# A macaron block on one Trainium2 core: the first feed-forward starts with a slot of 256 rows chosen from 512 tokens, the activation is rewritten, and the software DMA queue is drained inside the kernel

## What is computed

```python
x = x + 0.5 * ffn(layernorm(x))
x = x + attention(layernorm(x))          # 16 heads, recurrent "ABC" attention over chunks
x = x + 0.5 * ffn(layernorm(x))          # the same weights as the first

def ffn(x):                              # 2 experts, hidden size 2048
    probs = softmax(x @ w_router.T)
    e = argmax(probs); w = probs[e]
    h = x @ w_fc[e].T
    a = square(where(h >= 0, h, 0.5 * h))
    return w * (a @ w_proj[e].T)
```

## Time and profile before

| | |
|---|---|
| median of 3 runs | 2006.97 us (2006.1 to 2009.6) |
| the profiled execution's own time | 2002.07 us |
| its span, first to last instruction | 2000.3 us |
| mean granted TensorE clock | 0.992 of full speed |
| PE / weight loads / DVE / ACT / POOL busy | 95% / 80% / 70% / 33% / 14% |
| DMA over the span | 181.32 MB, 91 GB/s |

### The profile page before, as it was taken

The page is one execution under the profiler, slowest core; times in us unless marked ns, Lnnn a source line. Parts: engine busy times, 40 slices in busy tenths (PEclk is TensorE's granted clock), DMA queues, the critical chain, the costliest instruction groups (busy, mean ns, idle before and its releaser), DMA issues.

```text
span 2000.3 us, 29736 instructions
## 1 busy us (share of the span) xinstructions
PE 1904.3 (95%) x11600; PEld 1597.4 (80%) x11600; DVE 1398.1 (70%) x2733; ACT 653.9 (33%) x1176; POOL 279.5 (14%) x216
## 2 busy tenths in 40 slices
PE   2999999978999999999999999999999799999997
PEld 1788888867888888888888888888887588888885
DVE  5765667836777777777777777777778876665783
ACT  2544445524222222121222221221213244343561
POOL 3020101001111021020111110210201202010100
PEclk9999999999999999999999999999999899999999
DMA  6373445662112021121111120211211337333565
GB/s 231 128 214 123 107 152 172 191 193 77 30 40 40 12 59 22 19 53 25 25 45 28 40 41 12 59 22 20 53 17 38 131 115 217 123 101 122 171 191 167
DMA packets 189243, 181.32 MB, mean 91 GB/s; under 512 B 140336, under 2 KB 140336, under 8 KB 189104
## 3 DMA queue, kind: packets, MB, share of 16 engines
q1 hardware_dynamic: 181648, 162.09, 27.4%
q0 software_dynamic: 7456, 17.34, 4.2%
HBM read 137.40 MB, written 25.72 MB: 82 GB/s over the span
## 4 chain that ended last, share of the span: by engine, by line
PE 88%; DVE 6%; DMA 2%; ACT 2%; POOL 1%; issue 1%; SPq 0%; ACTq 0%; POOLq 0%; DVEq 0%
PE at_pj L1349 17%; PE at_pj L1323 14%; PE at_r L1414 8%; PE last_ff_ps_y L731 8%; PE last_ff_ps_h L285 8%; PE first_ff_ps_y L731 8%; PE first_ff_ps_h L285 8%; PE at_r L1493 3%; PE at_r L1481 2%; PE at_r L1398 1%; PE at_r L1445 1%; PE at_r L1515 1%; PE at_r L1457 1%; PE at_r L1486 1%; PE at_r L1450 1%; PE at_r L1439 1%
## 5 line engine op out<-in xcount | busy, mean ns | idle before, releaser
L1349 PE MATMUL at_pj<-at_w_lo,at_xT_hi 128*128 128x512 f32 x512 | 208.2, 407 | 0.0
L1349 PE MATMUL at_pj<-at_w_hi,at_xT_hi 128*128 128x512 f32 x512 | 200.3, 391 | 0.0
L1349 PE MATMUL at_pj<-at_w_hi,at_xT_lo 128*128 128x512 f32 x512 | 199.4, 390 | 0.0
L1323 PE MATMUL at_pj<-at_xT_hi,at_w_lo 128*128 128x512 f32 x384 | 156.7, 408 | 1.0 <-DVE at_xT_lo L1138 0.9
L1323 PE MATMUL at_pj<-at_xT_hi,at_w_hi 128*128 128x512 f32 x384 | 150.0, 391 | 0.0
L1323 PE MATMUL at_pj<-at_xT_lo,at_w_hi 128*128 128x512 f32 x384 | 149.7, 390 | 0.0
L621 DVE TENSOR_TENSOR last_ff_w_lo<-last_ff_stage,last_ff_w_hi 128x1024 fp32r<-128x1024 f32 x78 | 95.5, 1224 | 74.0 <-ACT last_ff_w_hi L429 74.0
L621 DVE TENSOR_TENSOR first_ff_w_lo<-first_ff_stage,first_ff_w_hi 128x1024 fp32r<-128x1024 f32 x78 | 95.5, 1224 | 72.0 <-ACT first_ff_w_hi L429 71.9
L920 POOL TENSOR_TENSOR at_w_lo<-at_stage,at_w_hi 128x1024 fp32r<-128x1024 f32 (+1 forms) x36 | 78.1, 2171 | 449.2 <-ACT at_w_hi L972 449.2
L1176 DVE TENSOR_TENSOR xres<-at_r,xres 128x512 f32<-128x512 f32 x128 | 88.5, 692 | 60.0 <-PE at_r L1414 58.9
L942 POOL TENSOR_TENSOR at_coef<-at_ms,minus_half 128x4 f32<-128x4 f32 x64 | 64.3, 1020 | 422.1 <-DVE at_ms L1284 422.1
(11 more groups left out here) (329 smaller groups left out, 4666.6 us busy)
## 6 DMA issues: line engine op xcount, KB each, us to landing
first_ff_stage<-wff SPq DMA_DIRECT2D x90, 512.0 KB, 4.3
last_ff_stage<-wff SPq DMA_DIRECT2D x90, 512.0 KB, 4.3
at_turned_ke<-at_ke_blocks SPq DMA_DIRECT2D x496, 32.0 KB, 2.0
at_stage<-watt SPq DMA_DIRECT2D x24, 512.0 KB, 3.8
at_stage<-watt SPq DMA_DIRECT2D x16, 384.0 KB, 3.4
xres<-x SPq DMA_DIRECT2D x4, 1024.0 KB, 9.9
mid_rows<-xres SPq DMA_DIRECT2D x4, 1024.0 KB
out<-xres SPq DMA_DIRECT2D x4, 1024.0 KB
```

The lines of the kernel that those rows point to most:

```text
L1323: last = pe.matmul(PJ[(7 * k + part) % 2][:, :], wq(w, kk, part), x[:, kk, tok], start=(kk == 0 and n == 0), stop=(kk == KC - 1 and n == 2))
L1349: last = pe.matmul(PJ[(7 * k + 3 + t) % 2][:, :], x[:, kk, tok], wvg(w, kk), start=(kk == 0 and n == 0), stop=(kk == KC - 1 and n == 2))
```

## The change

Four things are done at once.

1. **Widths and choice of the first feed-forward's slots.** `FIRST_WIDTHS` = 256, 512, 512, 512, 256, 128. Slot 0 is chosen after 512 tokens; so only group 0 is sorted and scattered before it. Group 1 is normed and scattered later, groups 2 and 3 follow in slot 0 and slot 1 (`last_slot` = 1: the last group's work stands in slot 1, where SP then waits at tile 12, for `late_slots` too). `late_slots` is rewritten for any widths. The second feed-forward keeps its widths.
2. **Group 0 in halves.** Its 4 tiles are loaded by 4 DMAs, and the statistics and roots are made for two tiles at a time; the same at the start of the attention, where also `split_lo(0)` stands ahead of the second unit's statistics on DVE and `project_s` ahead of `turn(1)` on PE.
3. **The activation.** ACT makes `half = 0.5 * h`, DVE `lean = max(h, half)`, ACT `a_hi` and `a`, both as Square of `lean`, DVE `a_lo`. The unsplit last slot has `half`, `lean`, and one Square.
4. **A drain inside.** POOL executes `pool.drain()` after slot 4's adds have landed, in both feed-forwards, ahead of the last slot.

The core of the diff:

```diff
-WIDTHS = (GROUP, GROUP, GROUP, GROUP // 2, GROUP // 2, P)
+FIRST_WIDTHS = (GROUP // 2, GROUP, GROUP, GROUP, GROUP // 2, P)
+LAST_WIDTHS = (GROUP, GROUP, GROUP, GROUP // 2, GROUP // 2, P)
...
-    at_once = [g for g in steps if g < 2]
-    with_slot = [g for g in steps if g >= 2]
+    at_once = [g for g in steps if g < 1]
+    with_slot = [g for g in steps if g == 1 or g == 2]
+    last_slot = 0 if early else 1
...
+    def parts(g):
+        if g == 0:
+            return ((1, slice(0, RT // 2)), (2, slice(RT // 2, RT)))
+        return ((g + 2, tiles(g)),)
...
             for t in range(RING, HT + RING):
-                if t == (3 if first_slot else 2) * RING:
+                if t == (3 if j <= last_slot else 2) * RING:
                     sp.wait_ge(x_turned, j * KC + KC)
                     sp.wait_ge(weight_done, j + 1)
...
-                            sp.wait_ge(scattered[2], 16 * RT)
+                            for g in with_slot:
+                                sp.wait_ge(scattered[g], 16 * RT)
                     else:
+                        if j == 1 and not early:
+                            sp.wait_ge(table_ready, KNOWN)
+                            tile0_next = sp.value_load(slot_table[0:1, 0, 2:3], min_val=0, max_val=HT)
                         sp.wait_ge(scattered[3], 16 * RT)
...
             for g in with_slot:
                 norm(g)
-        for g in with_slot:
-            scatter(g)
+            scatter(1)
+            norm(3)
+            scatter(2)
         def slot_body(j, width, after):
+            if j == 1 and not early:
+                scatter(3)
...
             pool.wait_ge(y_added, 16 * tiles_before[j + 1])
             pool.sem_inc(y_free, 1)
+            if j == EDGE - 1:
+                pool.drain()
...
-                act.activation(square[:, t % 2, 0:width], ps_h[t % 2][:, 0:width], ACT.Square).then_inc(square_done, 1)
+                act.activation(half[:, t % 2, 0:width], ps_h[t % 2][:, 0:width], ACT.Copy, scale=0.5).then_inc(half_done, 1)
...
-                act.activation(a_hi[:, t % RING, 0:width], a[:, t % 2, 0:width], ACT.Copy).then_inc(a_hi_done, 1)
+                act.activation(a_hi[:, t % RING, 0:width], lean[:, t % 2, 0:width], ACT.Square).then_inc(a_hi_done, 1)
+                act.activation(a[:, t % 2, 0:width], lean[:, t % 2, 0:width], ACT.Square).then_inc(a_done, 1)
...
-                dve.tensor_scalar(factor[:, t % 2, 0:width], ps_h[t % 2][:, 0:width], 0.0, 0.25, ALU.is_ge, ALU.max).then_inc(factor_done, 1)
-                dve.tensor_tensor(edge_a(t) if j == EDGE else a[:, t % 2, 0:width],
-                                  square[:, t % 2, 0:width], factor[:, t % 2, 0:width], ALU.mult).then_inc(a_done, 1)
+                dve.tensor_tensor(lean[:, t % 2, 0:width], ps_h[t % 2][:, 0:width], half[:, t % 2, 0:width], ALU.max).then_inc(lean_done, 1)
...
             statistics(0)
             dve.wait_ge(r_loaded, 16)
             step(dve.tensor_tensor(wdiff[:], rows[:, 0, :], rows[:, 1, :], ALU.subtract))
+            route(0)
             statistics(1)
-            route(0)
-            route(1, before=0)
+            place_step(0)
+            early_slot(dve, step, r, slot_table, 0, WIDTHS, RT, table_ready)
+            statistics(2)
+            route(1)
             place_step(1)
-            early_slot(dve, step, r, slot_table, 0, table_ready)
-            statistics(2)
-            statistics(3)
...
+            if not early and j == 0:
+                if t == 0:
+                    statistics(3)
+                if t == 2:
+                    route(2)
+                if t == 3:
+                    place_step(2)
+                    early_slot(dve, step, r, slot_table, 1, WIDTHS, 3 * RT, table_ready)
+            if j == last_slot:
+                if t == 4:
+                    step(gaps(3, range(3 * RT, 3 * RT + 2)))
+                if t == 5:
+                    step(gaps(3, range(3 * RT + 2, TILES)))
+                    choose(dve, step, r, tiles(3), is1_done)
+                    mark(3)
+                if t == (9 if early else 7):
+                    place_step(3)
+                if t == (10 if early else 8):
+                    late_slots()
...
             row_statistics(0)
+            split_lo(0)
             row_statistics(1)
-            split_lo(0)
...
             turned(0, 0, 1, k_mm)
+            project_s(0, 0)
             turn(1)
-            project_s(0, 0)
```

More of the change, by code:

```diff
@@ L149, in phase_feed_forward @@
     a_lo = sb("ff_a_lo", [P, RING, GROUP], F32R)
-    square = sb("ff_square", [P, 2, GROUP])
-    factor = sb("ff_factor", [P, 2, GROUP])
+    half = sb("ff_half", [P, 2, GROUP])
+    lean = sb("ff_lean", [P, 2, GROUP])
     a = sb("ff_a", [P, 2, GROUP])
@@ L174, in phase_feed_forward @@
     to_row = sb("ff_to_row", [P, 2, GT], I32)
-    in_loaded = [sem(f"rt_in_loaded{i}") for i in range(TILES // RT)] if x_in is not None else []
+    in_loaded = [None] + [sem(f"rt_in_loaded{i}") for i in range(1, TILES // RT)] if x_in is not None else []
     if x_in is not None:
@@ L323, in slot_body @@
                 return
-            if not first_slot:
+            if j > 1 or early and j > 0:
                 sp.wait_ge(table_ready, KNOWN)
@@ L360, in norm @@
         def norm(g):
[L361 to L364, removed]
+            for n, at in parts(g):
+                pool.wait_ge(var_ready, n)
+                pool.tensor_tensor(rstd[:, at], vare[:, at], c["minus_half"][:, at], ALU.pow).then_inc(rstd_done, 1)
+                pool.wait_ge(rstd_done, n)
+                pool.tensor_tensor(shift[:, at], nmean[:, at], rstd[:, at], ALU.mult).then_inc(shift_done, 1)
         def scatter(g):
@@ L457, in slot_body @@
                 if j == EDGE:
+                    if t == 0:
+                        act.wait_ge(a_lo_done, n)
+                    if t >= RING:
+                        act.wait_ge(down_done, n + 1)
+                    act.wait_ge(lean_done, n + 3)
+                    act.activation(edge_a(t), lean[:, t % 2, 0:width], ACT.Square).then_inc(a_done, 1)
                     continue
@@ L505, in gaps @@
                 dve.wait_ge(xn_done, i - steps[0] * RT + 1)
-                out = (square, square, factor, factor)[i % RT][:, i % 2, :] if g < 2 else rows[:, i % 2, :] if x_in is not None else xn_rest[:, i % 2, 0:D]
+                out = (half, half, lean, lean)[i % RT][:, i % 2, :] if g < 2 else rows[:, i % 2, :] if x_in is not None else xn_rest[:, i % 2, 0:D]
                 last = dve.tensor_tensor_reduce(out=out, in0=normed(i), in1=wdiff[:], scale=1.0, scalar=0.0,
@@ L556, in late_statistics, with beside @@
                 dve.tensor_scalar(vare[:, tiles(g)], mv[:, tiles(g), 1], EPS, None, ALU.add).then_inc(norms["var_ready"], 1)
-        def beside(t):
-            if early and t < 2:
+        def beside(j, t):
+            if early and j == 0 and t < 2:
                 late_statistics(t)
-            if 2 in with_slot and t == 1:
-                route(2)
-            if 2 in with_slot and t == 3:
-                place_step(2)
-                early_slot(dve, step, r, slot_table, 1, table_ready)
-            if t == 4:
-                step(gaps(3, range(3 * RT, 3 * RT + 2)))
-            if t == 5:
-                step(gaps(3, range(3 * RT + 2, TILES)))
-                choose(dve, step, r, tiles(3), is1_done)
-                mark(3)
-            if t == 9:
-                place_step(3)
-            if t == 10:
-                late_slots()
+            if not early and j == 0:
+                if t == 0:
+                    statistics(3)
[15 more added lines that the diff above has]
+                    late_slots()
@@ L675, in rank @@
             pe.matmul(ps_total[g], c["ones"][:], is1[:, tiles(g)], start=True, stop=True).then_inc(rank_mm, 1)
-        for g in at_once:
-            rank(g)
+        if not early:
+            rank(0)
+            rank(1)
         def turn_x(j, width, k0, k1, first=False):
@@ L1295, in pair @@
                         if k >= 2:
-                            early_slot(dve, step, routing, slot_table, k - 2, behind["table_ready"])
+                            early_slot(dve, step, routing, slot_table, k - 2, LAST_WIDTHS, k * UC, behind["table_ready"])
                     if more:
```

232 lines of the change are left out of this document (129 added, 103 removed).

## The result

The change makes the kernel slower: 2016.21 us (median of 6 executions, 2015.64 to 2017.84) against 2007.26 for the kernel before in the same comparison, ratio 1.0047 [1.0036, 1.0059]. Predicted was 1996.3, with a range of 1991 to 2003 and a chance of 0.08 for slower. The profiled execution took 2016.31 us, its span is 2014.6 us and its granted clock 0.985 of full speed.

What follows compares the result with a forecast made beforehand. PE was taken to bound the kernel (88% of the chain), its work unchanged. Start and slots −5.0, attention's start −0.5, drain −5.2, activation 0 sum to −10.7: 1991.4 on the profiled execution, 1996.3 as median, range 1991 to 2003.

Steps and rivals of the forecast that it cites:

- The start: Before the first slot matmul: earlier sorting, four scatters instead of eight and a shorter load save 9.6 us, to 34.2.
- Slot 0: First feed-forward, now 256 rows: 47.2 us without a stall plus 8.2 of stalls, 55.4; three waits for DVE's w_lo.
- Slot 1: First feed-forward: 88.9 us at 512 rows, plus 1.5 lost at tile 12 waiting for the last group.
- Slot 4: First feed-forward, 256 rows: following a 512-row slot, it takes 47.6 + 1.6 = 49.2 us.
- The activation: In the feed-forward slots: one pass moves from DVE to ACT; apart from DVE's relief in slot 0, 0 ± 1 us.
- The drain: At the kernel's end: with a drain inside, POOL's last DRAIN shrinks from 5458 ns to 0.25 us, −5.2 us.
- per-DMA reading: POOL's last DRAIN: it cleans up after each software DMA since the last one, 0.08 us each.
- The attention's start: First projection 1.55 us earlier, but ACT's queue sets the pace and fourth unit's rows start 0.5 earlier: −0.5 us.
- Rival 1: Kernel's end: the last DRAIN stays as it is, total gain −5.5, 2001.5 us; chance 0.24.
- Rival 2: Slots 0 and 1: weights land 2 to 3 us later, both tiles 12 miss, +5, 2001.3 us; chance 0.12.
- main case: Whole kernel: all terms as walked, including slot 1's 1.5 us loss at tile 12, 1996.3 us; chance 0.58.
- Rival 3: Slot 0 becomes bound by DMA, 14.7 MB in 55 us, making the kernel slower, 2015 us; chance 0.06.

Runs made afterwards that it cites:

- after_pad72: Changed kernel with a spare tensor of 72 numbers per partition instead of 80, putting later tensors back at their old addresses: 1998.72 us, ratio 0.9960.
- before_pad88: Kernel before with the spare tensor at 88 numbers instead of 80, moving everything allocated behind it by 32 bytes: 2023.29 us, ratio 1.0076.
- shift_all_32: Kernel before with an unused 32-byte tensor ahead of all weights and operands, so all move together: 2009.93 us, ratio 1.0006.
- late_stats: after_pad72 with statistics(3) of slot 0 at t = 6 instead of 0 and POOL's norm(3) behind scatter(2): 2001.69 us, ratio 0.9968.
- hold_tile14: after_pad72 with SP's wait in slot 1 put ahead of tile 14's load instead of tile 12's: 1997.02 us, ratio 0.9942.
- activation_only: Kernel before with the new activation alone (half, lean, a_hi and a as in the change): 2000.90 us, ratio 0.9957.
- spread: after_pad72 with group 2's sorting spread over slot 0's steps and SP's waits ahead of tile 14 in slots 0 and 1: 1991.08 us, ratio 0.9912.
- hold14_late_stats: after_pad72 with the edits of hold_tile14 and late_stats together: 1995.13 us, ratio 0.9935.

## Why the prediction was wrong

**The step that failed: "inside 512-row slots nothing but PE work counts, and this change doesn't alter the PE work", carried over to all other stages.** The prediction went on "what can move are the seams and the slots in which another engine is late", and so put the attention's steady state, over 1000 us of PE work, at nothing. The number of matmuls is the same, but not their pace. No term of the sum asked where the operands lie. after_pad72 and before_pad88 show that this missing term is +15 to +17.5 us, and shift_all_32 that it comes from a distance between tensors and not from the place of one (that of the weights and the operand that they meet, by the nearest reading). It alone turned the sign. The cause could be read from the code before the run: the widths change `BLOCKS`, which sets the size of a tensor.

Without that shift the change takes 1998.72, 2.4 us from the 1996.3 forecast, but partly by errors that cancel:

| term | predicted | measured |
|---|---|---|
| first slot matmul | 34.2 | 35.4 |
| slot 0 | 55.4 | 57.1 |
| slot 1 with its tile 12 | 90.4 | 95.4 |
| slots 2 and 3 | 176.9 | 176.9 |
| slot 4 | 49.2 | 47.4 |
| end of the first feed-forward against before | −5.0 | +1.0 |
| activation | 0 | −8.6 [−11.9, −5.2] by the runs alone, 3.7 of it located |
| attention's start | −0.5 | −0.6 [−2.4, +1.4] by the runs alone |
| drain | −5.2 | −4.6 [−7.2, −2.2] by the runs alone |
| operands' distance | none | +17.5 (13 to 22), 15.2 (11 to 20) in before_pad88 |

(The slots are those of the kernel after; after_pad72 has 35.4, 56.2, 93.7, 176.9 and 47.8, and ends 0.9 us before the kernel before.)

- **The start** came 1.2 late: `row_i` at 18.4 instead of 17.4, and the last scatter landed 5.67 after its issue where I carried over 4.82; the load and the turn were as walked.
- **Slot 0.** Two waits of PE for DVE's `w_lo`, 2.4 us at `up(3)` and 2.1 at `up(6)`, where I had three of 7.3 in all; the one at `up(5)`, for `route(2)`, didn't come. But the granted clock was 0.94 over 57.1 us, some 3.4 us more, for which I had no term beyond the 0.9 for clock and first split. 47.2 + 0.9 + 4.5 + 3.4 makes 56.0; the last 1.1 wasn't traced. The first wait was as much ACT's as the statistics' (late_stats).
- **Slot 1.** The walk to tile 12 was right to 1.6 us: I had the landing 59.3 after the slot's start, it was 60.9 (153.4 − 92.5), and `up(12)` fell due at 60.5, where I had 60.2. `late_slots` ended at 51.3 as walked (51.5); SP then took 2.0 instead of 0.8, and the load 7.6 instead of 7. The wait was 2.8. What the sum lacked is what follows a wait, 3.2 us at half the clock; hold_tile14 took away both.
- **Slot 4** doesn't lose at its head what the old slot 3 lost; the new activation won 0.8 of it in the same place (activation_only, 49.3 for 50.1); the other 1.9 weren't traced.
- **The activation** wasn't neutral. I gave DVE's relief to the walk of slot 0 and put the rest at 0 ± 1. The traces show gains where DVE was late, in both feed-forwards: PE's waits for DVE go from 5.6 to 3.0 us in the first and from 3.8 to 2.7 in the second. Over half of the −8.6 stays open.
- **The drain** was right by the per-DMA reading. The Trainium skill ("VectorE: DVE Perf Modes", section "The DRAIN you can't avoid") has about 12 ns for the DRAINs of preamble and postamble on all five engines. The trace doesn't agree for POOL's at the block's end, which took 119 ns behind one software DMA and 5458 behind 66.
- **The attention's start**: the first projection came 2.0 earlier (I had 1.55), the fourth unit's rows 0.2 later instead of 0.5 earlier. That it is worth next to nothing was right; the −0.5 itself is less than the runs can tell.
- **The rivals.** Rival 1 (the last DRAIN stays) is wrong. Rival 2 (landings 2 to 3 us later, in both slots) didn't come: slot 0 has no wait for loads, and in slot 1 the wait was 1.3 longer than in the main case. Rival 3 (slot 0 bound by DMA) is wrong: the queues carried 270 GB/s at a share of 0.77. The result was on the slower side by none of the three.

## What to carry to other kernels

A tensor that grows moves all that is allocated behind it, and 512-column matmuls on fp32r operands changed their pace here when one operand moved against the other by 32 bytes: fix the addresses before two versions are compared, and compare the pace of the code that wasn't touched first. A wait of PE of two to three microseconds can cost as much again in half clock behind it; it did so in the kernel after, and not in late_stats, so give it a range. In a narrow slot put extra work in one piece per step on each engine, and drain the queue of software DMAs where its engine is idle anyway.

## What the runs showed of the hardware that was not expected

- Matmuls of 512 columns started every 229 ns with the operands at the old distance and every 233 ns at 32 bytes more, both at a granted clock of 1.00 and with PE busy for 999.22 of 1000 us. Matmuls of 128 columns, and 512-column ones whose two operands had moved together, kept their pace. Six attention units took 206.1 to 206.3 us at the old distance (three kernels), 209.1 at +32 bytes (two), 207.8 at −64 bytes (one).
- A wait of 2.8 us of PE in a slot that had run at 2.4 GHz was followed by 12 matmuls in 5.49 us instead of 2.72. After waits of 1.7 us and less (spread) the granted clock stayed at 1.00. In between it went both ways: waits of 2.4 (the kernel after) and 2.3 us (after_pad72) at `up(3)` were followed by 0.64 over the next 4.7 us, waits of 2.7 (late_stats) and 2.9 us (hold14_late_stats) at the same place by 1.00.
- A DRAIN of POOL took 82 ns for each software DMA since the last one.
- The attention as a whole, from its first projection to the second feed-forward's first matmul, took 1136.6 us before, 1140.2 in after_pad72 and 1143.3 in shift_all_32, with equal times for the six units (within 0.2 us); with the operands shifted it took 1158.3 (the kernel after) and 1156.9 (before_pad88). Part of that lies at its start, where PE has waits: between 440 and 480 us the granted clock was 0.83 in the first two and 0.74 in the third, by estimate 0.09 × 40 = 3.6 us. The rest wasn't traced.
